# Maximum passes of a four-layer graph network on one core: PE's loop over pairs of groups written out, with constants in its waits

## The reference

```python
def _gin_layer(h, src, dst, W, b):
    msgs = h[src]
    agg = jax.ops.segment_max(msgs, dst, num_segments=N_NODES)
    agg = jnp.where(jnp.isfinite(agg), agg, jnp.zeros_like(agg))
    return (h + agg) @ W + b
x = _gin_layer(h, src, dst, W1, b1)
x = jax.nn.relu(x)
x = _gin_layer(x, src, dst, W2, b2)
```

## Time and profile before

| what | value |
|---|---|
| median of 3 runs | 6553.22 us (6550.06 to 6576.66) |
| the profiled execution | 6574.14 us |
| its span, first to last instruction | 6572.5 us |
| busy share of the span: PE, DVE, ACT, POOL | 35%, 69%, 38%, 59% |
| first maximum pass, groups 2 to 55 | 4530 to 5426 us |
| second maximum pass, groups 2 to 55 | 5581 to 6509 us |

### The profile page before, as it was taken

The page is one execution under the profiler, slowest core; times in us unless marked ns, Lnnn a source line. Parts: engine busy times, 40 slices in busy tenths (PEclk is TensorE's granted clock), DMA queues, the critical chain, the costliest instruction groups (busy, mean ns, idle before and its releaser), DMA issues.

```text
span 6572.5 us, 44667 instructions
## 1 busy us (share of the span) xinstructions
PE 2285.5 (35%) x14635; PEld 1383.5 (21%) x14635; DVE 4554.9 (69%) x5458; ACT 2521.1 (38%) x3136; POOL 3883.7 (59%) x3861
## 2 busy tenths in 40 slices
PE   3997500000010000000100000035888783877876
PEld 2775300000000000000100000013444441444443
DVE  7978587777767777777687777774666653656654
ACT  2340144444323444443244433433444442444443
POOL 1001277777747777775577777716666555655664
PEclk7998755555555555555555555557999895988987
DMA  1233454444435444443454444412333332333332
GB/s 63 81 121 137 136 162 158 149 149 148 155 114 171 159 151 149 149 154 126 143 168 149 150 153 150 146 46 86 111 103 111 103 100 75 111 101 101 103 101 88
DMA packets 262138, 826.79 MB, mean 126 GB/s; under 512 B 72362, under 2 KB 109274, under 8 KB 258115
## 3 DMA queue, kind: packets, MB, share of 16 engines
q0 software_dynamic: 165280, 426.11, 22.6%
q1 hardware_dynamic: 96679, 398.78, 16.8%
HBM read 492.30 MB, written 341.93 MB: 127 GB/s over the span
## 4 chain that ended last, share of the span: by engine, by line
POOL 38%; PE 27%; issue 21%; DVE 7%; ACT 2%; another core or an unknown queue 2%; DMA 1%; SPq 0%; DVEq 0%; POOLq 0%; ACTq 0%
POOL arena L2327 37%; PE pair_ps L1874 20%; PE pair_ps L1971 4%; DVE outs L925 1%; PE banks_ps L1949 1%; ACT outs L1712 1%; PE banks_ps L1840 1%; DVE outs L1003 1%; DVE work L1153 0%; PE pair_ps L1883 0%; DVE bn_st L703 0%; PE pair_ps L1987 0%; ACT arena L1690 0%; POOL H L2327 0%
## 5 line engine op out<-in xcount | busy, mean ns | idle before, releaser
L2327 POOL DMA_INDIRECT arena<-table,src_i x3596 | 3633.4, 1010 | 1766.9 <-issue 1251.5
L1852 PE MATMUL pair_ps<-ident,tails 128*128 128x128 f32 x9 | 2.7, 439 | 3366.7 <-DVE tails L1260 2242.1
L1874 PE MATMUL pair_ps<-bias,arena 128*128 128x384 bf16 x4050 | 790.9, 345 | 312.9 <-issue 261.7
L1098 DVE TENSOR_TENSOR pair_ps<-pair_ps,arena 128x1792 f32<-128x1792 f32 x168 | 341.4, 2032 | 711.2 <-DMA arena<-table,src_i 481.9
L1874 PE MATMUL pair_ps<-work,arena 128*128 128x384 bf16 x4050 | 754.2, 337 | 162.3 <-issue 161.0
L1003 DVE TENSOR_TENSOR_SCAN outs<-arena,banks_ps 128x1920 f32<-128x1920 f32 x112 | 465.1, 4153 | 496.4 <-ACT banks_ps L1698 471.6
L1852 PEld LDWEIGHTS pair_ps<-ident,tails 128*128 128x128 f32 x9 | 1.5, 213 | 3369.0 <-DVE tails L1260 2243.8
L1153 DVE TENSOR_TENSOR_SCAN work<-work,banks_ps 128x1920 f32<-128x1920 f32 x168 | 697.6, 4153 | 5.8
L1578 ACT ACTIVATE LD<-DE 128x112 f32<-128x112 f32 x168 | 49.8, 296 | 1423.4 <-issue 647.6
L1874 PEld LDWEIGHTS pair_ps<-bias,arena 128*128 128x128 bf16 x4050 | 405.3, 101 | 679.2 <-issue 465.9
L1598 ACT COPY outs<-work 128x1792 f32<-128x1792 f32 x171 | 541.8, 3170 | 0.0
(11 more groups left out here) (320 smaller groups left out, 4382.8 us busy)
## 6 DMA issues: line engine op xcount, KB each, us to landing
rows_att<-outs SPq DMA_DIRECT2D x165, 1008.0 KB
rows_plain<-outs SPq DMA_DIRECT2D x110, 896.0 KB
arena<-table,src_i POOLq DMA_INDIRECT x3596
kept_counts<-arena SPq DMA_DIRECT2D x15, 2000.0 KB, 6.4
bias<-sources SPq DMA_DIRECT2D x108, 192.0 KB
arena<-kept_counts SPq DMA_DIRECT2D x10, 2000.0 KB, 8.3
outs<-kept_counts SPq DMA_DIRECT2D x5, 2000.0 KB, 7.7
qchunks<-qtable SPq DMA_DIRECT2D x3, 3136.0 KB
```

Source lines behind the costliest of these rows:

```text
L1098: chain(v.tensor_tensor(prod, prod, ring[:, s, :, 0:D], ALU.mult))
L1874: ins = pe.matmul(picked_ps[g % 2], parts3[:, a, t, :], hots_made[g % 2][:, :, t, :], start=t == a == 0, stop=t == NB - 1 and a == 2)
L2327: pool.indirect_dma_start(dst, None, tab, bass.IndirectOffsetOnAxis(ap=idx, axis=0))\
```

## The change

The parameter `it` and `await_count` go. `pick` and `turn_picked` wait on constants in every group, and `pick_rows` calls `pick` for all of groups 2 to 55 one after another. The values that are awaited, their order and all matmuls are as before; PE's program has 100 more group bodies (50 for each pass).

```diff
-            def await_count(semaphore, value, each, it):
-
-                if it is None:
-                    pe.wait_ge(semaphore, value)
-                else:
-                    pe.wait_ge(semaphore, it * each + value)
-                    pe.nop(nofuse=True)
-
-            def pick(k, g, it=None):
-
-                await_count(s_onehot, made_group(k, g) + 1, 2, it)
+            def pick(k, g):
+
+                pe.wait_ge(s_onehot, made_group(k, g) + 1)
                 for t in range(NB):
                     if t == TURN_AT and g > PICK_FROM:
-                        turn_picked(k, g - 1, it)
+                        turn_picked(k, g - 1)
...
-            def turn_picked(k, g, it=None):
-
-                await_count(s_whole, made_group(k, g) + 1, 2, it)
-                await_count(s_spread, scanned(k, g - 2), 2, it)
+            def turn_picked(k, g):
+
+                pe.wait_ge(s_whole, made_group(k, g) + 1)
+                pe.wait_ge(s_spread, scanned(k, g - 2))
...
                 pe.wait_ge(s_vec, MARK[f"parts{k}"])
-                first = PICK_FROM
-                for g in range(first, first + 2):
+                for g in range(PICK_FROM, GROUPS):
                     pick(k, g)
-                with pe.Fori(0, (GROUPS - first) // 2 - 1) as it:
-                    for g in range(first + 2, first + 4):
-                        pick(k, g, it)
                 turn_picked(k, GROUPS - 1)
```

## The result

| | kernel before | written out |
|---|---|---|
| median (20 executions each) | 6558.36 us (6539.54 to 6576.66) | 6582.43 us (6557.71 to 6603.36) |
| ratio, 95% interval | | 1.0035, 1.0025 to 1.0045 |
| the profiled execution | 6574.14 us | 6603.36 us |
| its span | 6572.5 us | 6601.7 us |

What follows compares the result with a forecast made beforehand. The prediction took POOL's gathers, and PE coming free 2.1 us after them, to bound each group. All terms were taken as 0, so it forecast 6553 us, range 6520 to 6586, with 8 in 10 for 6480 to 6620.

Steps and rivals of the forecast that it cites:

- What bounds the kernel: Maximum passes: a group takes 13.5 us of gathers, 2.1 until PE comes free, 1.0 to the next gather: 16.6 us.
- The loop doesn't make PE crawl: PE's matmuls start singly with pauses (crawl) beside POOL's gathers; straight-code group 2 crawls worst, so no loop is needed.
- A plain group still has 16.6 us: Sign in the changed profile: ordinary groups' scans stay 16.6 us apart, ACT's line 1697 starting 2.1 us after POOL's last gather.
- Code and fetches, 0 us: PE's added group bodies: 1.0 MB and 61 packets more, taken as 0 us; 119 us if each were waited for.
- The fused waits, 0 us: Constant waits stand with PE's instruction instead of ahead of it, same semaphores, values and order: 0 us.
- the sequencer's share: PE's removed waits, additions and loop ends: 30 us of sequencer time, taken as hidden, 0 us; bounds 0 to -30 us.
- more costly pairs: Slower rival: early transposes bring more pairs (a short, then a long scan interval, 5.4 us each): 6607 us; chance 0.14.
- Timing shifts, 0 us: Transposes may move some 0.1 us against the gathers, changing how often pairs come: 0 us, ends 64 less and 54 more.
- no pairs at all: Favourable end of the timing shifts: every group of both loops plain, 880 us a loop, 64 us less.
- All other stages are untouched: Stages outside the two maximum passes, some 4600 us, were taken as unchanged.

Runs made afterwards that it cites:

- e12: Kernel before, POOL gathering 2 of 11 steps in groups 2 to 55 of the maximum passes, in a session with the crawl: 6003.8 us in one execution.
- e3: Changed kernel with all three waits of a group on instructions of their own, constants still: 6572.65 us, 1.0023 against the kernel before.
- e4: Kernel before with 26 groups in the loop's body and 2 rounds, register waits kept: 6563.06 us, 1.0020 against the kernel before.
- e9: Changed kernel as it is, run again in the third session, with the crawl: 6609.81 us, 1.0017 against the kernel before.
- e1: Changed kernel as it is, run again in the first session, with the crawl: 6583.02 us, 1.0041 against the kernel before.
- e2: Changed kernel with only the wait for `s_onehot` at each group's head on an instruction of its own: 6585.24 us, 1.0048 against the kernel before.
- e11: Kernel before with 4 groups in the loop's body and 13 rounds, third session, with the crawl: 6599.67 us, 1.0008 against the kernel before.
- e10: Kernel before plus 1.0 MB of PE matmuls that are never run, third session, with the crawl: 6601.83 us, 1.0008 against the kernel before.
- e7: Kernel before with 4 groups in the loop's body and 13 rounds, second session, no crawl: 5849.89 us, 1.0000 against the kernel before.

## Why the prediction was right and wrong

**What bounds the kernel: right.** Groups close on the gathers and on PE's coming free after them. The changed kernel has the same sequence in its plain group, and e12 moves the distance to 12.5 us by leaving out gathers.

**The loop doesn't make PE crawl: right.** It was read from the earlier trace rows, and group 2, e3 (constants, all apart) and e4 (registers) bear it out.

**"A plain group still has 16.6 us": not the kernel's number.** 16.8 us in the first session, 16.65 in e9, the same code; and 16.8 in e4 with its register waits. The 0.15 us lie between POOL's last gather and ACT's line 1697 (mean 2.2 us in the first session, 2.0 in e9, for the 2.1 promised). They belong to chip and session. Over the 106 intervals of both passes they make 16 us, as much as the passes of the two first profiles differ by, so these can't be subtracted from each other.

**Code and fetches, 0 us: right where it could be isolated.** 115 packets were promised, 116 came. Without the crawl they cost nothing (0.9999 and 1.0000), where the upper bound was 119 us. With the crawl e4 fetches as much and lies no higher than e3. The Trainium skill ("Runtime: NRT & Kernel Launch", "Instruction fetch mechanics") would have kernels unrolled to spare fetches at branches; neither 1.0035 with the crawl nor 1.0000 without shows a gain.

**The fused waits, 0 us: this step failed.** The prediction saw that PE "may have more matmuls in hand when the crawl ends" and put that at 0, and it bounded the sequencer's share between 0 and -30 us, so neither term allowed a loss. With the crawl, taking the second wait off the transposes again, onto an instruction of its own, is worth 14 us (e1 and e2 against e3), about half of the 29 us by which the two lie above the kernel before in their session (means). That this half comes by way of more pairs, as in the rival "more costly pairs" (chance 0.14, 54 us), is likely from 15 pairs against 10 and 8 but not shown: the third session has 23 to 25 whatever the waits are. The other half stays open.

**Timing shifts, 0 us: sized from too little, and the direction is not borne out.** The kernel before had 5 and 11 pairs in its passes, the changed one 9 and 6: no more in sum, and 59 and 56 us above plain groups. One profiled execution can't give the count, whose scatter shows in the times (37 us between the fastest and slowest of 20 executions of the kernel before). The prediction held that early transposes make a pair, and they do. It also held that PE, relieved of work, brings them earlier. In plain groups they start 9.2 us behind the scan in the kernel before, 10.0 in the changed one, 9.9 and 9.8 in e1 and e2, 9.6 and 9.5 in e3 and e4 (means, each within some 0.3): if anything, later with fused waits. The end "no pairs at all" was mis-sized as well: the last two intervals of each pass are some 11 us, since gathers are running out there, so 16 pairs at 5.4 us are 86 us and not 64.

**"All other stages are untouched": the 15 us follow the session.** Outside the two passes the kernel before took 4749 us in its first profile and the changed one 4764. But all four kernels of the first session took 4764 to 4765 there, and in the third session the changed kernel took 4747 and e11 with its loop 4747 too. So nothing here puts them down to the code; what is missing is a profile of the kernel before from the first session.

**Open.** Why a wait fused with the transposes leads to a longer time is not known; where the transposes start in plain groups does not explain it. The part of the cost that e3 and e4 keep (0.2%) is unexplained; size of the program alone is not shown to cost (e10: 1.0008, 0.9991 to 1.0025), and fetches beside a crawl were not tried without other changes. Nor was it found what makes a session crawl.

## What to carry to other kernels

Where an engine's instructions are answered late because of something else (here a row of gathers), taking sequencer work away from it brought nothing here, and the place of one wait a group, 51 ns long where it stands apart, was worth 14 us of 6557. Such a term has no price that can be added up from the instructions' own durations. A count that scatters from pass to pass in one profile (5 and 11 pairs) is a term with two ends and needs profiles of both kernels from the same chip and session, several of each. Writing out the loop for constant waits cost 0 to 0.4% here; to shorten these passes, gathers would have to come out of the row (leaving out 9 of 11, as e12 does at the price of wrong maxima, took 591 us off); spreading them was not tried.

## What the runs showed of the hardware

- The same kernel took 6558, 5851, 6595, 5836 and 5836 us in five sessions, the second and third on one chip. The difference is the crawl: 516 idle spots of weight loads against 77 in the changed kernel's second pass, plain groups 16.7 against 13.9 us, the attention passes 1057 to 1061 against 972 to 974 us. A gather on POOL takes 1010 against 956 ns in the mean.
- Beside a row of gathers single matmuls come 0.7 to 3.5 us apart and PE's semaphores are answered late, until 2.0 to 2.3 us after the last gather of a plain group. Two gathers in a row are not enough for it (e12), while in the same execution group 2 crawls beside 34.
- Without the crawl, 62 more instruction packets (1.0 MB) cost less than 6 us of 5836.
- A loop body of 4 groups (about 40 KB) runs 13 rounds twice with 3 packets more than one of 2 groups (e7, e11: 57 against 54), so it is not fetched again. One of 26 groups is fetched in each round (e4: 122 packets), and its jump back takes 3.5 to 3.7 us in place of 0.2.
